# A gated four-stage block on one Trainium2 core: eight experts computed for every token, or the two chosen ones on rows sorted by expert

## What is computed

```python
probs = softmax(xf @ Wr)                     # xf: layer-normalised x, 4096 tokens; 8 experts
topk_p, topk_i = top_k(probs, 2)
# for each token and each of its two experts e: (xf @ Wi[e]) @ Wo[e], 256 -> 256 -> 256
out = sum over the two of topk_p * that
x = x + tanh(g_ffn[0]) * out
```

## Time and profile before

| | us |
|---|---|
| median of the runs | 1144.22 (1143.49 to 1146.84, 3 runs) |
| profiled execution | 1147.13 |
| its span, first to last instruction | 1145.2 |
| stage A, up to the first transposition of stage B | 163.8 |
| stage B, up to the first transposition of stage D | 240.6 |
| stage D with C inside it | 740.8 |

### The profile page before, as it was taken

The page is one execution under the profiler, slowest core; times in us unless marked ns, Lnnn a source line. Parts: engine busy times, 40 slices in busy tenths (PEclk is TensorE's granted clock), DMA queues, the critical chain, the costliest instruction groups (busy, mean ns, idle before and its releaser), DMA issues.

```text
span 1145.2 us, 14891 instructions
## 1 busy us (share of the span) xinstructions
PE 1094.8 (96%) x5194; PEld 865.2 (76%) x5194; DVE 538.0 (47%) x1420; ACT 449.8 (39%) x805; POOL 120.8 (11%) x164
## 2 busy tenths in 40 slices
PE   7989979899999989999999999999999999999997
PEld 5757767677777757887887787788787788788886
DVE  6567656777777672243334235136134333422411
ACT  1344431013233244445435435435434443543532
POOL 0025552200000030010010010001001001001001
PEclk9989989999999989999999999999999999999999
DMA  9200000620110030000000000000000000000000
GB/s 343 95 1 1 1 1 1 250 82 0 37 37 0 1 147 1 1 18 2 1 19 1 1 1 20 1 0 19 1 1 19 1 1 19 1 1 1 19 1 21
DMA packets 5480, 33.31 MB, mean 29 GB/s; under 512 B 1198, under 2 KB 1454, under 8 KB 3368
## 3 DMA queue, kind: packets, MB, share of 16 engines
q1 hardware_dynamic: 4584, 29.41, 6.6%
q10 hardware_dynamic: 832, 3.02, 0.7%
HBM read 28.23 MB, written 4.19 MB: 28 GB/s over the span
## 4 chain that ended last, share of the span: by engine, by line
PE 84%; DVE 6%; ACT 4%; issue 3%; POOL 1%; DMA 1%; DVEq 0%; SPq 0%; POOLq 0%; ACTq 0%
PE psum L857 52%; PE psum L740 13%; PE psum L763 2%; PE psum L750 1%; PE psum L475 1%; PE psum L562 1%; PE psum L538 1%; PE psum L789 1%; PE psum L771 1%; PE psum L718 1%; PE psum L576 1%; DVE x_residual L1571 1%; DMA x_residual<-in_x 1%; PE psum L592 1%; ACT L1130 1%
## 5 line engine op out<-in xcount | busy, mean ns | idle before, releaser
L857 PE MATMUL psum<-hidden_a_high,mlp_rest_rounded 128*128 128x512 f32 x512 | 207.6, 405 | 0.0
L857 PE MATMUL psum<-hidden_b_high,mlp_h_rounded 128*128 128x512 f32 x512 | 200.6, 392 | 0.0
L857 PE MATMUL psum<-hidden_a_low,mlp_rest_rounded 128*128 128x512 f32 x512 | 199.8, 390 | 0.0
L857 PE MATMUL psum<-hidden_b_low,mlp_h_rounded 128*128 128x512 f32 x512 | 199.2, 389 | 0.0
L1685 DVE TENSOR_TENSOR hidden_a_low<-hidden_a,hidden_a_high 128x512 fp32r<-128x512 f32 x128 | 92.3, 721 | 173.9 <-ACT hidden_a_high L1195 173.1
L1685 DVE TENSOR_TENSOR hidden_b_low<-hidden_b,hidden_b_high 128x512 fp32r<-128x512 f32 x64 | 44.3, 692 | 221.2 <-ACT hidden_b_high L1195 221.2
L1571 DVE SCALAR_TENSOR_TENSOR x_residual<-psum,expert_weight,x_residual 128x256 f32 (+1 forms) x256 | 107.2, 475 | 41.1 <-PE psum L740 40.3
L857 PEld LDWEIGHTS psum<-hidden_a_high,mlp_rest_rounded 128*128 128x128 f32 x512 | 96.2, 188 | 24.2 <-issue 3.6
L857 PEld LDWEIGHTS psum<-hidden_a_low,mlp_rest_rounded 128*128 128x128 f32 x512 | 96.2, 188 | 22.2 <-issue 3.3
L857 PEld LDWEIGHTS psum<-hidden_b_high,mlp_h_rounded 128*128 128x128 f32 x512 | 96.1, 188 | 19.9
L857 PEld LDWEIGHTS psum<-hidden_b_low,mlp_h_rounded 128*128 128x128 f32 x512 | 96.1, 188 | 19.9
(11 more groups left out here) (214 smaller groups left out, 1635.4 us busy)
## 6 DMA issues: line engine op xcount, KB each, us to landing
x_residual<-in_x SPq DMA_DIRECT2D x4, 1024.0 KB, 23.9
mlp_h_slice<-in_h SPq DMA_DIRECT2D x4, 1024.0 KB, 4.9
mlp_rest<-in_h SPq DMA_DIRECT2D x1, 4096.0 KB, 20.2
mlp_h<-in_h SPq DMA_DIRECT2D x1, 4096.0 KB, 12.6
out<-x_residual SPq DMA_DIRECT2D x8, 512.0 KB, 2.6
mlp_rest<-in_w SPq DMA_DIRECT2D x3, 1024.0 KB, 9.1
expert_in<-in_Wi SPq DMA_DIRECT2D x1, 2048.0 KB, 16.0
expert_out<-in_Wo SPq DMA_DIRECT2D x1, 2048.0 KB, 20.5
```

Of the source, the lines that this page charges most:

```text
L857: last = mm(o, a, b, start=(k == 0 and i == 0), stop=(k == n_k - 1 and i == len(parts) - 1))
```

## The change

Stage B is rebuilt around rows in DRAM. For each batch of 1024 tokens:

- **Route** (`r_norm`, `r_turn`, `r_logits`, `r_copy` to `r_tiles`): the eight tiles are normalised into a buffer of the batch (`xm`), turned in pairs, and multiplied by the router. VectorE marks the two chosen experts; two matmuls with a triangle and with ones count, for each token and expert, the tokens ahead of it (`r_rank`). From the counts come each token's two slots, in an order sorted by expert with every expert starting at a tile of 128, and the expert's column for each of the 23 tiles (`eid`).
- **Scatter** (`scatter`, GpSimd): 16 indirect DMAs a batch, each writing 128 rows of 1 KB from `xm` to `slots` in DRAM; SP has cleared `slots` before, 3.1 MB a batch.
- **Experts** (`s_turn`, `s_high`, `s_low`, `s_experts`, `s_save`): the slots come back in chunks of four tiles (SP, 24 loads of up to 512 KB), each pair of tiles is turned, split into high and low, and multiplied by one expert of 256 columns, whose column is taken from a register; registers are filled from `eid`, 12 or 11 at a time. Each tile needs six matmuls of 256 columns. ScalarE copies the result out and stores it by chunks (24 stores). 48 turns of this loop, q = 0 to 47, of 92 tiles in all.
- **Gather** (`gather`, GpSimd): 8 indirect DMAs a group bring the two rows of each token back, and VectorE adds them with their weights (`add_rows`). Groups 0 and 1 are added within the loop, groups 2 to 7 within stage D.

Around it: the test of the weights moves into stage A, 22 slices of 1024 columns that SP loads and ScalarE examines; the weights of the MLP are then loaded a second time by GpSimd's queue into fp32r tiles, so that the rounding by ScalarE and GpSimd falls away.

```diff
+            def s_experts(q, columns):
+                pe.wait_ge(xsl_r, q + 1)
+                if q >= 2:
+                    pe.wait_ge(ye_r, q - 1)
+                for i in range(pair_tiles(q)):
+                    v = columns[(q % PAIRS * 2 + i) % 12]
...
+                    for k in range(KC):
+                        mm(o, xsh[:, q % 3, k, t], wexp_h[:, k, bass.ds(v, D)], start=(k == 0), stop=False)
+                        mm(o, xsl[:, q % 3, k, t], wexp_h[:, k, bass.ds(v, D)], start=False, stop=False)
+                        last = mm(o, xsh[:, q % 3, k, t], wexp_l[:, k, bass.ds(v, D)], start=False, stop=(k == KC - 1))
...
-            with pe.Fori(0, NG // 2 - 1) as i:
-                b_pass(2 * i + 1, 1, 2 * i)
-                b_pass(2 * i + 2, 0, 2 * i + 1)
-            b_last_pass(NG - 1, 1)
+            s_turn(0)
+            s_turn(1)
+            for q in range(NP):
+                if q % PAIRS % 6 == 0:
+                    columns = s_columns(q // PAIRS, q % PAIRS // 6)
+                if q + 2 < NP:
+                    s_turn(q + 2)
+                s_experts(q, columns)
...
+            sp.wait_ge(ex_ps, 1)
+            sp.dma_start(tri[:], d["tri"]).then_inc(tri_in, 16)
+            sp.dma_start(iota[:], d["iota"]).then_inc(tri_in, 16)
+            for b in range(B):
+                dst = slots[b].rearrange("(c p j) d -> p c (j d)", c=NCK, j=CHUNK)
+                sp.dma_start(dst, d["zeros"].unsqueeze(1).broadcast_to([P, NCK, CHUNK * D])).then_inc(fill_done, 16)
...
+            for c in range(B * NCK):
+                if c % NCK == 0:
+                    sp.wait_ge(sc_done[c // NCK], 16 * 2 * JT)
+                if c >= 2:
+                    sp.wait_ge(xt_ps, min(pairs_before(c - 2) + 2, c // NCK * PAIRS if c % NCK < 2 else NP))
+                else:
+                    sp.wait_ge(r2_ps, 2 * B)
+                n = chunk_tiles(c)
+                sp.dma_start(xs[:, c % 2, 0:n, :], chunk_rows(slots, c, n)).then_inc(xs_in[c % 2], 16)
...
+            pool.wait_ge(ix_r, 2)
+            scatter(1, ALL)
+            pool.wait_ge(ix_r, 3)
+            scatter(2, ALL)
+            for h in range(2):
+                pool.wait_ge(st_done[h], 16 * NCK // 2)
+            gather(0, yg0)
+            pool.wait_ge(ix_r, 4)
+            scatter(3, ALL)
             invert(0, G, STATS_A + 1)
+            pool.wait_ge(cb_r, G)
+            gather(1, yg0)
+            for n, done in (("w1", w12_in), ("w2", w12_in), ("h1", h1_in), ("w3", h1_in)):
+                pool.dma_start(mlp_r[n], d[n]).then_inc(done, 16)
             invert(G, G, STATS_A + 2)
...
             invert(0, G, 1, stats_c, inv_c)
+            pool.wait_ge(y_ps, NP)
+            pool.dma_start(mlp_r["h2"], d["h2"]).then_inc(h2_in, 16)
```

More of the change, by code:

```diff
@@ L1164, in _ @@
[L1164 to L1179 removed]
+            s_high(0)
@@ L1794, in _ @@
[L1794 to L1799 removed]
+            pool.wait_ge(y_ps, NP)
+            pool.dma_start(mlp_r["h2"], d["h2"]).then_inc(h2_in, 16)
+            for h in range(2):
+                pool.wait_ge(st_done[h], 16 * B * NCK // 2)
+            for n in range(NG):
+                if n + 2 < NG:
+                    pool.wait_ge(sb_ps, n + 2)
+                    gather(n + 2, yg)
+                if n + 1 < NG:
+                    invert(G * (n + 1), G, n + 2, stats_c, inv_c)
+                if n + 2 < NG:
+                    invert(G * (n + 2), G, STATS_A + 3 + n)
@@ L1879 @@
     d["out"] = nc.dram_tensor("out", (NG, P, G, D), F32, kind="ExternalOutput").ap()
+    for n in ("slots", "yrows"):
+        d[n] = [nc.dram_tensor(f"{n}_{b}", (ROWS_B, D), F32, kind="Internal").ap() for b in range(B)]
     program(nc, d)
```

911 lines of the change are left out of this document (586 added, 325 removed).

## The result

The changed kernel took 1188.04 us (median of 4 runs, 1186.35 to 1190.17) where the kernel before took 1143.91 us in the same session: 1.038 times as long, with a 95% interval of 1.0355 to 1.0407. The forecast was 1116 us with a range up to 1170, so both the sign and the range missed. The profiled execution has a span of 1184.5 us, 39.3 more than before's 1145.2, at a granted clock of 0.921 (before 0.984).

What follows compares the result with a forecast made beforehand. TensorE's matmuls were taken to bound stage B. Loop work of 141 us plus 15 of waits, starting at 216, brought stage D 30 us earlier; with 2 added in stage D, the median was 1116 us, range 1080 to 1170.

Steps and rivals of the forecast that it cites:

- Clearing: Stage A: clearing 12.6 MB of slots costs nothing at 333 GB/s, 30 us at half that; taken as 8 us.
- Routing of batch 0: Stage A, passes of batches 2 and 3: TensorE 6 us, VectorE 15 with about half in idle time; 10 us.
- The sums of batch 3: Before the loop: VectorE's 26 us set the pace over GpSimd's 24 (t, one indirect DMA's hold, 1.2); loop starts 27 later.
- the port rule weighed in the prediction: VectorE's fp32 normalisations lock GpSimd and its DMA descriptors out of shared ports; scatters held up at most 11 us, mostly hidden.
- TensorE's work in the loop: Loop of 48 turns: experts, turns, routing, stage C of group 0, registers and their loads sum to 141 us.
- Registers: Loop, TensorE: register instructions and addresses 9 us, bounds nothing to +54; eight loads of 11 or 12 registers 8 us.
- Waits in the loop: Loop: VectorE's routing, chunk loads, stores and the pipeline's first fill cost TensorE 15 us, range 5 to 30.
- The rival on the DMA engines: Loop: some 40 MB take 120 us at 333 GB/s, hidden, but 200 us at 200 GB/s; +44, 1160 us, chance 0.08.
- Converting loads slow: MLP weights: at 52 GB/s w1 to h1 end 70 us late and h2 another 40; 1226 us, chance 0.08.
- Register addresses slow for each product: Loop: register-addressed matmuls take 0.217 us instead of 0.136; +45, 1161 us, chance 0.08.
- Clearing slow: Stage A: clearing the slots from DRAM to DRAM is slow; +22, 1138 us, chance 0.10.
- GpSimd's queue binds: Sums and loop: at 2.6 us per indirect DMA, scatters and gathers delay TensorE; +43, 1159 us, costing from 1.5; chance 0.12.

Runs made afterwards that it cites:

- e10_one_pause: The changed kernel with a single pause: the second eight scatters of batch 1 wait for the fifth pair of tiles; 1142.7 us, 0.998 of the kernel before.
- r2_two_bank_pairs: The changed kernel with scatters spread, batch 0's last ten between batch 3's additions, and batch 3's sums on two PSUM bank pairs; 1136.9 us, 0.990 of before.
- e6_loads_kept: The changed kernel with fixed columns for 11 of 12 tiles, all eight register loads kept, each with one tile using its register; 1182.8 us, 1.033 of before.

## Why the prediction was wrong, point by point

**Stage A up to its last scores.** Forecast 28 us later, measured 26.4 (187.6 against 161.2). Slices 10 forecast, 10.3 measured. Their mechanism was the one named, and one more: with two buffers, each pair of reads waits for the next loads (5.11 and 3.91 us on the chain, and the loads take 3.9 to land):

```profile
96.39 5.11 DMA mlp_slice<-in_w
```

Clearing 8 forecast, 0 measured: it ran at some 327 GB/s, the rate of the low bound. Routing of batch 0, 10 forecast: without the slices pass two grew by 7.5 us over before (37.9 against 30.4) and the pass behind it by 10.0 (29.7 against 19.7), 17.5 in all. In that third pass VectorE works 25.2 us, 10.7 more than before, which I had half hidden, and TensorE waits for it, 5.6 us at one place of the changed kernel:

```profile
PE psum L746 <- DVE update_of_sub2char L1631: 5.6, 1, 5.6
```

So the near hit of the total is luck: 8 us too much for the clearing against 7.5 too little for the routing.

**The sums of batch 3: 27 forecast, 50.4 measured.** The time of one scatter was right: 0.96 us and 0.30 between two, 1.27, where I took 1.2. The Trainium skill, "DMA: Bandwidth & Descriptors", section "Anatomy of one DMA — SWDGE (gpsimd) path", has the larger part of such a DMA's fixed 2 us in its completion. The trace agrees on that (in e10_one_pause a scatter of batch 0 lands 2.4 us after its issue begins and holds GpSimd for 0.96 of them), but the hold isn't small. Near the normalisations one scatter took 1.48 us (186.88), in the direction of the port rule weighed in the prediction, at 0.5 us a time. The step that failed is the one after: I compared GpSimd's total, 10t + 12, with VectorE's total and let the larger set the pace. Work in a queue doesn't add like that. All ten scatters stood ahead of one addition, so VectorE stopped:

```profile
205.38 0.96 POOL L2079 DMA_INDIRECT slots<-x_norm_of_even_batch,slots_of_tokens  x1 [0.30 <-issue]
206.35 0.74 POOL L2098 TENSOR_TENSOR x_residual<-x_residual,update_of_char2sub 128x256 f32<-128x256 f32 x1
```

```profile
195.01 0.73 DVE L1473 TENSOR_SCALAR x_norm_of_odd_batch<-x_residual,ln_mean_var,ln_rstd 128x256 f32<-128x256 f32 x2
208.03 0.42 DVE L1629 SCALAR_TENSOR_TENSOR update_of_char2sub<-gate_tanh,psum 128x256 f32<-128x256 f32 x1 [12.29 <-issue]
```

Interleaving gave 8.2 us of it back. The rest is two omissions. The sums use one pair of banks, so each went through TensorE, ScalarE and VectorE before the next began, 3.8 to 3.9 us, with TensorE at its 1.2 GHz level (granted clock 0.50 from the first sum to the loop). It fell to that level at 178.9 us, in the 5.6 us in which TensorE stood waiting for VectorE, and stayed there even in r2_two_bank_pairs, where TensorE is busy in 26.0 of the sums' 26.7 us; 22.9 was reached in an execution whose clock was 0.72 there. And between the start of the last sum and the loop stand 13.0 us in which VectorE works 11.8: ranks, slots, six measurements. My 26 us for VectorE were right (26.1 by the rows), but I laid them all beside the sums, and these can only follow them; in VectorE's list they stand ahead of the first split of slot rows, so the loop waits for them too.

**TensorE's work in the loop: 141 forecast, 132.1 measured** between the first and last expert product, of which part at the lower clock; 120.2 in e10_one_pause. Registers: 9 + 8 forecast; with the stalls out of the way, fixed columns are worth 10 to 12 us (ratios 0.989 and 0.987 against 0.998, the first known to 0.006). The eight loads took 1.06 to 5.29 us each in e10_one_pause, against one of 0.49 in the rows of before. Right in size, a little high, as far as the intervals tell.

**Waits in the loop: 15 forecast, 68 measured.** The loop term as a whole was 156, plus 2 to stage D's turn; with the one pause it measured 152.2 (244.3 to 396.5). So the step that failed is that the list of waits was taken as complete. It had chunks, stores and VectorE's routing, all of them semaphores that I could see in the program. The stalls brought another 52 us in these two executions (40 to 45 in the medians), in which TensorE's matmuls and counts came late without a wait in the program that explains it. That 152 is near 158 is in part luck: without the stalls TensorE works 120.2 us where I took 141, and stands 27.4 between the first and last expert product where I took 15. "What a matmul with a register in its address costs beyond that no row shows" was the right warning in the wrong place: I bounded it as a price for each product, 0 to 54 us, and the true price was nothing for each product and 40 to 45 us for a combination with the burst.

**The collision with the weights.** The rival on the DMA engines counted 40 MB over the loop and found them hidden. The total was fine, the placing was not: 7 MB issued in 2 us took a chunk's load from 3 to 15 us, and TensorE was busy 7.6 of 15.5 us there. The first line is the chain's piece, the second the page's issue of h1, with KB and us to landing:

```profile
394.55 14.97 DMA slot_rows<-slots
```

```profile
mlp_rest_rounded<-in_h POOLq DMA_DIRECT2D x1, 4096.0 KB, 22.0
```

**The rivals.** Converting loads slow: fell, 4 MB of h1 landed in 22.0 and h2 in 14.1 us. Register addresses slow for each product: fell, 0.12 us apart. Clearing slow: fell. GpSimd's queue binds: t was 1.27, below its point of 1.5, and yet the queue did bind once, by order and not by length. None of the rivals was what happened. Both of my signs of being wrong about the whole came true: stage A grew by 74.2 us (the loop from 163.8 to 238.0) against the limit of 60, and a turn cost 204.3 / 48 = 4.26 us against 3.9.

**Stage D.** Forecast +2.0, measured +1.4.

In sum, 1117.2 + 23.4 for the sums + 46.3 for the loop - 1.4 - 0.6 for the rest gives the 1184.5 of the profile, within 0.4. Had the stalls not come, the change would have been 1143 us, a quarter of a per cent below before: the rest of the forecast gain went into the sums of batch 3.

## What to carry to other kernels

In a queue, cost what stands ahead of the work that others wait for, not the queue's total against another engine's; and ask of each piece of preparation whether it can lie beside the work or only behind it. Where a change brings two things that no row of the profile shows, here bursts of indirect DMAs and registers in TensorE's addresses, leave room for what they do together and try the change with each one missing; here one wait in the burst was enough to remove it. Before a wait is called nobody's, look up who counts that semaphore up. A transfer that is hidden by its total can still stand in front of the one load that nothing hides, so large loads belong where no first chunk is waited for.

## What the runs showed of the hardware that was not expected

With the experts' columns in registers of TensorE and 16 indirect DMAs in a row from GpSimd at the loop's start, TensorE started 13 matmuls in 13 us and 7 in 14 us where undisturbed ones start 0.12 us apart, its semaphore counts came up to 28 us after the matmul's end by the rows, and ScalarE stood on them for up to 14.2 us. A single pause after eight of the 16, 3.9 us long, removed this from all four bursts, and leaving out the registers did as well; in `e6_loads_kept` it also held up matmuls without a register in their address. The traces of the stalled executions lack landing records from 181 us on, before either condition comes into play. The cause was not found.

An indirect DMA of 128 rows of 1 KB holds GpSimd for 0.96 us, with 0.30 to the next. A load of 11 or 12 registers held TensorE's sequencer for 1.05 to 5.29 us, the longer ones behind a full queue of products. Clearing 12.6 MB from DRAM to DRAM went at 327 GB/s.
